# Zero matmuls beside the folding of the maxima, the row of maxima copied by bank, and TensorE's last part moved into the branch

## The chip, the cores and the metric

The kernel runs on one core of a Trainium2 chip. The core has five engines that run side by side and meet through semaphores: TensorE (matmuls, with a queue of its own for weight loads), VectorE, ScalarE, GpSimd and SyncE, which here only issues transfers. The metric is the device time of one execution in microseconds, lower is better.

## The reference

The program is one layer of a Perceiver. 128 queries of width 256 attend to a context of 12544 rows, then to themselves, and then go through a gated feed-forward part whose weights and activations are rounded to integer grids. Cut to what is computed:

```
x = x + cross_attention(layernorm(x), ctx, ctx, mask)   # 16 heads of 16, softmax over 12544 keys
x = x + self_attention(layernorm(x))                    # 16 heads of 16, causal, 128 keys
x = x + ffn(layernorm(x))                               # 256 -> 768 gate and up -> 256, quantized

# cross attention
qh, kh, vh = (q @ Wq.T + bq), (k @ Wk.T + bk), (v @ Wv.T + bv)    # each (.., 16, 16)
scores = einsum('bqhd,bkhd->bhqk', qh, kh) / 4 ; masked -> -1e7
out = einsum('bhqk,bkhd->bqhd', softmax(scores), vh)

# ffn
x = act_qdq(x);  up = act_qdq(x @ Wup.T);  gate = act_qdq(x @ Wgate.T)
gate = act_qdq(gate * round_u16(sigmoid(gate)));  o = act_qdq(gate * up);  return o @ Wdown.T
```

`act_qdq` needs the largest absolute value of its whole argument before it can round.

## The kernel before, in words

The 12544 context rows are 98 tiles of 128, in 14 blocks of 7. The order of work is written out by hand for every engine; nothing is scheduled by a planner.

**First pass** (to 244 us of the profile). For each block TensorE projects keys and values (L811, L820) and scores all queries against all keys once (L852, `score_for_max`), only to find each query's and head's largest score. VectorE takes part of these maxima straight (L626) and folds the rest, copied by ScalarE (L442), into a running array `running` of 16 heads by 448 keys (L629). Keys and values go to DRAM.

**The fold.** When the last block is scored, VectorE folds `running` by halves (L654, three steps), reduces it (L657), joins it with `row_max` (L658) and writes the negative, `neg_max` (L661). TensorE turns its 16 columns into one row of partition 96 of `ps_a`, 16 matmuls of 128 columns over four banks (L927). ScalarE copies banks 0 and 1 of that row into `q_stack` (L480), VectorE banks 2 and 3 (L665). With this row in `q_stack`, and ones in the matching row of `k_stack`, a score comes out of the matmul with the maximum already subtracted. The matmul of zeros at L934 clears `attended`, the bank in which the second pass sums.

**Second pass.** A block is 56 score matmuls in 8 units of 6 and 8 by turns (`score`, L946). Their result goes through an exponential on ScalarE (L492, four slots of probabilities) and is multiplied with the values (`add_up`, L960: 12 or 16 matmuls a unit, each of which the profile counts twice). TensorE waits for two exponentials, scores two more units, and then adds up the two. Units 14 and 15 of the last pair of blocks have nothing left to score. The loop over the pairs (L992) runs six times, and the seventh pair is written out behind it.

**The branch.** Whether any key is masked is known only at run time. TensorE loads a flag (L896) and has the two passes twice in its program, without masks and with them, each in an `If` (L996 to L998). Here nothing is masked, so the first is run. What comes behind both branches stands once: a matmul of one element (L1000) whose semaphore `sums_done` lets VectorE copy the sums (L688), four transposes of them (L1003), the normalization, the self-attention, the output projection, and the feed-forward part up to L1112.

**Zero matmuls.** `keep_clock(bank, count)` (L860 to L863) runs matmuls of zeros, 512 columns each, into a bank that nobody needs. Their counts stand in `WARM`; the first, 15, is run while VectorE normalizes the sums.

**Self-attention.** Queries and keys, then values are projected (L1020, L1028). Four groups of four heads are scored (L1036, L1038), exponentiated by ScalarE (L512, L515), turned (`turn_probs`, L1045), copied, and multiplied with the values (`attend_self`, L1053). ScalarE copies the values at L500, ahead of its first exponential.

**Feed-forward.** The peaks found by VectorE are spread over all partitions by TensorE (`spread_peaks`, L1079), and VectorE waits for them (`scales`, L743 to L749).

## Time and profile before

| | us |
|---|---|
| median of 3 timed runs | 521.67 (520.98 to 522.05) |
| the profiled execution, its own time | 524.74 |
| its span, first to last instruction | 523.0 |
| TensorE busy | 481.6 (92% of the span) |
| ScalarE busy | 375.9 (72%) |
| VectorE busy | 294.9 (56%) |
| mean granted clock of TensorE, as a share of 2.4 GHz | 0.951 |

The durations below come from the profiled execution, whose time is 3.07 us above the median of the timed runs. The times at which rows start are in us from the start of its span. A busy TensorE is not one at its peak: its matmuls are pipelined, and a row with x16 gives the time from the first start to the last end. "Idle before" in brackets names what ended the wait; "issue" means that nothing the profile shows was waited for. The granted clock of TensorE has two levels, 1.2 GHz (0.5) and 2.4 GHz (1.00); a value between them means that it changed inside the stretch. A matmul of zeros of 512 columns takes twice as long at the lower one.

### The profile page before, as it was taken

The page shows a single profiled execution, that of the slowest core. Times are in us where ns is not written, and L with a number is a line of the kernel's source. Part 1 is how long each engine was busy: PE and PEld are TensorE (multiplying, and loading weights), DVE is VectorE, ACT ScalarE, POOL GpSimd, SP SyncE. Part 2 cuts the span into 40 slices and gives each one's busy share as a digit, 9 for nine tenths or more (in the row PEclk, how much of TensorE's full clock was granted, in tenths as well). Part 3 has the DMA queues.
Part 4 walks back from the last instruction along what each step waited for, and adds up shares of the span by engine and source line. Part 5 has one row for each costly group of instructions (what it writes and reads, how often), then busy time and mean ns, then how long its engine had stood idle before and what let it go on. Part 6 is the DMA issues. An engine that isn't in the chain of part 4 may idle for free.

```text
span 523.0 us, 14251 instructions
## 1 busy us (share of the span) xinstructions
PE 481.6 (92%) x5620; PEld 381.0 (73%) x5620; DVE 294.9 (56%) x425; ACT 375.9 (72%) x410; POOL 101.2 (19%) x101
## 2 busy tenths in 40 slices
PE   6889999999999999993699999999999999959997
PEld 3867777777777776771589899898998998829443
DVE  6757999999999999999389100000000000036575
ACT  3248888888888888874489999899999999705011
POOL 5684322233332233305000000000000000000000
PEclk9879999999999999996599999999999999979699
DMA  8735676766677666958937777888777774000000
GB/s 278 248 130 205 270 303 253 266 234 230 241 291 298 237 263 233 391 233 305 410 103 275 285 269 290 303 303 301 278 267 264 262 278 170 5 3 1 0 0 10
DMA packets 34759, 117.47 MB, mean 225 GB/s; under 512 B 4400, under 2 KB 10416, under 8 KB 34736
## 3 DMA queue, kind: packets, MB, share of 16 engines
q1 hardware_dynamic: 30560, 110.58, 56.0%
q0 software_dynamic: 4032, 6.42, 4.3%
q8 instruction: 17, 0.28, 0.2%
q10 hardware_dynamic: 144, 0.13, 0.1%
q14 instruction: 6, 0.05, 0.0%
HBM read 74.44 MB, written 39.47 MB: 218 GB/s over the span
## 4 chain that ended last, share of the span: by engine, by line
PE 54%; DVE 30%; issue 10%; ACT 4%; DMA 1%; DVEq 1%; SPq 0%; ACTq 0%
PE ps_a L946 20%; PE ps_k L960 17%; DVE block_max L626 14%; DVE early L629 7%; PE ps_k L811 4%; PE ps_a L820 2%; PE ps_a L863 2%; DVE k_lo L587 2%; ACT early L442 1%; PE ps_a L852 1%; DMA v_in<-in_wv 1%; PE ps_a L1053 1%; DVE early L654 1%; PE ps_a L889 1%; PE ps_a L1091 1%
## 5 line engine op out<-in xcount | busy, mean ns | idle before, releaser
L626 DVE TENSOR_REDUCE block_max<-ps_a 128x2 f32<-128x896 f32 x112 | 121.1, 1083 | 1.8 <-PE ps_a L852 1.7
L946 PE MATMUL ps_a<-q_stack,k_stack 128*128 128x256 f32 x784 | 112.0, 295 | 1.3 <-DVE q_stack L665 0.8
L946 PEld LDWEIGHTS ps_a<-q_stack,k_stack 128*128 128x128 f32 x784 | 100.2, 192 | 13.7 <-issue 11.4
L442 ACT CAST early<-ps_a 128x896 bf16<-128x896 f32 x104 | 93.9, 903 | 8.0 <-PE ps_a L852 8.0
L492 ACT ACTIVATE middle<-ps_a 128x1536 f32<-128x1536 f32 (+1 forms) x56 | 90.3, 1663 | 13.1 <-PE ps_a L946 13.1
L688 DVE COPY early<-ps_k 128x512 f32<-128x512 f32 x1 | 0.7, 692 | 171.6 <-PE ps_a L1000 171.6
L492 ACT ACTIVATE early<-ps_a 128x1536 f32<-128x1536 f32 (+1 forms) x56 | 90.2, 1662 | 7.8 <-PE ps_a L946 7.8
L348 POOL TENSOR_TENSOR k_stack<-early,k_stack 128x448 fp32r<-128x448 f32 x52 | 59.2, 1143 | 122.6 <-DVE early L629 113.6
L820 PE MATMUL ps_a<-w_hi,k_stack 128*128 128x256 f32 x392 | 69.8, 302 | 0.0
L629 DVE TENSOR_TENSOR early<-early 128x896 bf16<-128x896 bf16 x104 | 68.0, 654 | 0.0
L811 PE MATMUL ps_k<-k_stack,w_hi 128*128 128x448 f32 x224 | 61.8, 398 | 6.2 <-DVE v_in L619 3.9
L820 PEld LDWEIGHTS ps_a<-w_hi,k_stack 128*128 128x128 f32 x392 | 54.6, 194 | 11.9 <-issue 11.7
L852 PE MATMUL ps_a<-k_hi,q_pad 32*128 32x448 f32 x448 | 54.5, 476 | 8.5 <-ACT early L442 7.7
L426 ACT ACTIVATE k_hi<-ps_k,bk 128x448 fp32r<-128x448 f32 x56 | 35.5, 634 | 32.0 <-PE ps_k L811 32.0
L811 PEld LDWEIGHTS ps_k<-k_stack,w_hi 128*128 128x128 f32 x224 | 38.7, 193 | 21.0 <-DVE k_lo L587 11.4
L960 PE MATMUL ps_k<-early,v_in 128*17 128x128 f32 x1568 | 48.2, 273 | 0.7 <-ACT early L492 0.7
L960 PE MATMUL ps_k<-middle,v_in 128*17 128x128 f32 x1568 | 48.3, 273 | 0.0
L852 PEld LDWEIGHTS ps_a<-k_hi,q_pad 32*128 32x128 f32 x448 | 22.1, 186 | 34.8 <-issue 23.4
L587 DVE SCALAR_TENSOR_TENSOR k_lo<-ps_k,bk,k_hi 128x448 fp32r<-128x448 f32 x56 | 38.1, 680 | 13.3 <-ACT k_hi L426 10.8
L960 PEld LDWEIGHTS ps_k<-early,v_in 128*17 128x17 f32 x1568 | 40.4, 97 | 4.6 <-ACT early L492 1.0
L960 PEld LDWEIGHTS ps_k<-middle,v_in 128*17 128x17 f32 x1568 | 40.4, 97 | 3.8
L432 ACT COPY early<-ps_a 128x512 f32<-128x512 f32 (+1 forms) x56 | 30.1, 537 | 15.6 <-PE ps_a L820 12.9
(172 smaller groups left out, 428.9 us busy)
## 6 DMA issues: line engine op xcount, KB each, us to landing
k_stack<-k_hi_scratch SPq DMA_DIRECT2D x56, 448.0 KB, 6.1
v_scratch<-early SPq DMA_DIRECT2D x14, 952.0 KB, 6.1
v_in<-v_scratch SPq DMA_DIRECT2D x14, 952.0 KB, 8.0
early<-in_ctx SPq DMA_DIRECT2D x14, 896.0 KB, 5.6
k_hi_scratch<-k_hi SPq DMA_DIRECT2D x28, 448.0 KB, 3.7
k_lo_scratch<-k_lo SPq DMA_DIRECT2D x28, 448.0 KB, 3.8
k_stack<-k_lo_scratch SPq DMA_DIRECT2D x28, 448.0 KB, 6.4
mask_b<-in_maskn POOLq DMA_DIRECT2D x14, 224.0 KB, 5.6
```

Source lines behind the costliest of these rows:

```text
L348: nc.gpsimd.tensor_tensor(ctx_lo[:, par, c, half], ctx_t[:, c * BK:(c + 1) * BK][:, half], ctx_hi[:, par, c, half].bitcast(f32), ALU.subtr ...
L426: nc.scalar.activation(k_hi[:, par, m, n * HK:(n + 1) * HK], ps_k[:, 0:HK], ACT.Identity, bias=bk[:, m:m + 1]).then_inc(hi_ready, 1)
L442: nc.scalar.copy(staged[:, u % 2], pair_scores(u, 0)).then_inc(max_copied, 1)
L492: nc.scalar.activation(probs[u % SLOTS_P][:, 0:width], ps_a[:, UNIT_BANK[u % 2]:UNIT_BANK[u % 2] + UP[u % 2] // 2, :].rearrange("p a n -> ...
L587: nc.vector.scalar_tensor_tensor(k_lo[:, m, half], ps_k[:, 0:HK], bk[:, m:m + 1], k_hi[:, par, m, half].bitcast(f32), ALU.add, ALU.subtrac ...
L626: nc.vector.tensor_reduce(block_max[:, par, 2 * u:2 * u + 2], pair_scores(u, 1), AX.X, ALU.max).then_inc(max_taken, 1)
L629: nc.vector.tensor_tensor(copied_rows(u), copied_rows(u), staged[:, u % 2], ALU.max).then_inc(run_taken, 1)
L811: last = nc.tensor.matmul(ps_k[:, 0:HK], w[:, 0, c, m * P:(m + 1) * P], part[:, par, c, n * HK:(n + 1) * HK], start=(k == 0), stop=(k == l ...
L820: last = nc.tensor.matmul(ps_v[:, n * D:(n + 1) * D], part[:, par, c, t * P:(t + 1) * P], w[:, 1, c, :], start=(j == 0), stop=(j == len(te ...
L852: last = nc.tensor.matmul(outs[-1], q_pad[rows, head, :], k_hi[rows, par, m, keys], start=True, stop=not masked, skip_group_check=True)
L946: last = nc.tensor.matmul(ps_a[:, bank, (k % 2) * 2 * Q:(k % 2 + 1) * 2 * Q], k_stack[:, b_par, a, t * P:(t + 1) * P], q_stack[:, a, :, :] ...
L960: last = nc.tensor.matmul(attended[32 * j:32 * j + VW, c * Q:(c + 1) * Q], v_ring[:, b_par, t, h, :], probs[slot][:, k * Q:(k + 1) * Q], s ...
```

## The change

- **The fold.** Behind the last `score_for_max` TensorE runs 24 matmuls of zeros into `attended` (`WARM_FOLD`), and then waits for `neg_max`.
- **The row of maxima.** The 16 matmuls signal after each four (one bank) and not after each eight. VectorE copies banks 0 and 2, ScalarE banks 1 and 3, 512 elements each and not 1024. The first scores wait, pair of heads by pair of heads, for the bank that holds their part of the row (`wait_max_row`), and not for the whole row.
- **The last two units.** In the last pair of blocks TensorE waits for the exponential of unit 14 before it adds up unit 14, and for that of unit 15 before it adds up unit 15, and not for both at first.
- **The end of the branch.** Everything TensorE does behind the branches stands in a function `finish()` that is called at the end of either branch. The matmul of one element is gone: VectorE waits for the last `add_up` itself (`prob_slots_free`).
- **The sums** are copied in two halves, and a half's transposes wait for that half alone.
- **The values of the self-attention** are projected behind the turning of groups 0 and 1, into bank 1 of `ps_a`, and no longer ahead of the scores. ScalarE copies them behind its third group. The values' first product now stands behind the turning of group 2, the other three behind the turning of group 3; before, two stood on either side.
- **VectorE's `scales(3, 2, 12)`** stands behind the first step on the sigmoid, and not ahead of the wait for it.

```diff
+WARM_FOLD = 24
@@ ScalarE
-            act.wait_ge(max_rows_ready, 1)
             act.wait_ge(q_spread, 8)
-            nc.scalar.mul(q_stack[SR:SR + 1, 0:PR // 2, :, :].rearrange("p a b q -> p (a b q)"),
-                          ps_a[SR:SR + 1, 0:2, :].rearrange("p a q -> p (a q)"), 1.0).then_inc(max_rows_set, 1)
+            for n in (1, 3):
+                act.wait_ge(max_rows_ready, n + 1)
+                nc.scalar.mul(q_stack[SR:SR + 1, 2 * n:2 * n + 2, :, :].rearrange("p a b q -> p (a b q)"),
+                              ps_a[SR:SR + 1, n, :], 1.0).then_inc(odd_rows_set, 1)
...
-            act.wait_ge(v2_projected, 1)
-            nc.scalar.copy(v2_sb[:, :, 0:HD], ps_k[:, D:2 * D].rearrange("p (h d) -> p h d", h=H)).then_inc(v2_copied, 1)
...
                 if g == 2:
                     copy_odd(1)
+                    act.wait_ge(v2_projected, 1)
+                    nc.scalar.copy(v2_sb[:, :, 0:HD], ps_a[:, 1, 0:D].rearrange("p (h d) -> p h d", h=H)).then_inc(v2_copied, 1)
@@ VectorE
-            dve.wait_ge(max_rows_ready, 2)
             dve.wait_ge(q_spread, 8)
-            nc.vector.tensor_scalar(q_stack[SR:SR + 1, PR // 2:PR, :, :].rearrange("p a b q -> p (a b q)"),
-                                    ps_a[SR:SR + 1, 2:4, :].rearrange("p a q -> p (a q)"), 1.0, None,
-                                    ALU.mult).then_inc(max_rows_set, 1)
+            for n in (0, 2):
+                dve.wait_ge(max_rows_ready, n + 1)
+                nc.vector.tensor_scalar(q_stack[SR:SR + 1, 2 * n:2 * n + 2, :, :].rearrange("p a b q -> p (a b q)"),
+                                        ps_a[SR:SR + 1, n, :], 1.0, None, ALU.mult).then_inc(even_rows_set, 1)
...
-            dve.wait_ge(sums_done, 1)
-            nc.vector.tensor_copy(sums_sb, attended).then_inc(sums_copied, 1)
+            dve.wait_ge(prob_slots_free, NB * UNITS + SLOTS_P)
+            for half in range(2):
+                nc.vector.tensor_copy(sums_sb[:, half * D:(half + 1) * D], attended[:, half * D:(half + 1) * D]
+                                      ).then_inc(sums_copied, 1)
...
-            scales(3, 2, 12).then_inc(up_scale_ready, 1)
             dve.wait_ge(sig_ready, 1)
             link(nc.vector.tensor_scalar(sig, sig, 65536.0, MAGIC, ALU.mult, ALU.add))
+            scales(3, 2, 12).then_inc(up_scale_ready, 1)
@@ TensorE
                 for u in range(LAG, NG):
                     score_for_max(NB - 1, 1, u, masked)
+                pe.wait_ge(lo_ready, NB * DC * 2)
+                keep_clock(attended, WARM_FOLD)
 
                 pe.wait_ge(row_max_ready, NB + 1)
...
-                    if h % HT == HT - 1:
+                    if h % 4 == 3:
                         last.then_inc(max_rows_ready, 1)
-                pe.wait_ge(lo_ready, NB * DC * 2)
                 nc.tensor.matmul(attended, zeros_b[:, 0:P], zeros_b[:], start=True, stop=True,
                                  skip_group_check=True).then_inc(prob_slots_free, SLOTS_P)
-                pe.wait_ge(max_rows_set, 2)
...
+                def wait_max_row(a):
+                    pe.wait_ge(odd_rows_set if a // 2 % 2 else even_rows_set, a // 4 + 1)
...
+                        if opening and t == 0 and a % 2 == 0:
+                            wait_max_row(a)
...
                     for u in range(0, 2 * UNITS, 2):
+                        ending = final and u == 2 * UNITS - 2
                         for w in (u, u + 1):
-                            pe.wait_ge(exp_done, i * (2 * UNITS) + w + 1)
-                            if not (final and u == 2 * UNITS - 2):
+                            if not ending:
+                                pe.wait_ge(exp_done, i * (2 * UNITS) + w + 1)
...
                         for w in (u, u + 1):
+                            if ending:
+                                pe.wait_ge(exp_done, i * (2 * UNITS) + w + 1)
                             add_up(w // UNITS, w % UNITS, w % SLOTS_P)
...
+            def finish():
+                for c in range(4):
+                    pe.wait_ge(sums_copied, c // 2 + 1)
+                    last = nc.tensor.transpose(ps_x[:, c * P:(c + 1) * P], sums_sb[:, c * P:(c + 1) * P], eye[:])
+                last.then_inc(sums_turned, 1)
...
+                turn_probs(0)
+                turn_probs(1)
+                for c in range(DC):
+                    last = nc.tensor.matmul(ps_a[:, 1, 0:D], xt[:, c, :], wqvk[:, c, D:2 * D], start=(c == 0), stop=(c == DC - 1))
+                last.then_inc(v2_projected, 1)
+                turn_probs(2)
+                pe.wait_ge(v2_copied, 1)
+                attend_self(0)
+                turn_probs(3)
+                attend_self(1)
+                attend_self(2)
+                attend_self(3).then_inc(self_attended, 1)
...
             for masked in (False, True):
                 with pe.If(masked_flag == int(masked)):
                     attend(masked)
-
-            nc.tensor.matmul(ps_v[0:1, 0:1], zeros_b[:, 0:1], zeros_b[:, 0:1], start=True, stop=True).then_inc(sums_done, 1)
-            pe.wait_ge(sums_copied, 1)
...
+                    finish()
```

What the order of the instructions shows follows for three places, all on TensorE. Lines of the changed program are a few higher: its L856 is L852 before, L867 is L863, L932 is L927, L937 is L934, L953 is L946, L967 is L960, L1009 is L1003, L1015 is L1009, L1026 is L1020, L1046 is L1045, L1054 is L1053 and L1061 is L1028.

TensorE before, between the last scoring of the first pass (L852) and the first scores of the second:

```order
L852 MATMUL ps_a<-k_hi,q_pad 128x448 x3
L927 MATMUL ps_a<-eye_b,neg_max 1x128 [waits row_max_ready]
L927 MATMUL ps_a<-eye_b,neg_max 1x128 x15
L934 MATMUL ps_k<-zeros_b 128x512 [waits lo_ready]
L946 MATMUL ps_a<-q_stack,k_stack 128x256 [waits consts_set,q_spread,stack_in0,v_evacuated,max_rows_set]
L946 MATMUL ps_a<-q_stack,k_stack 128x256 x13
```

The same place in the changed program:

```order
L856 MATMUL ps_a<-k_hi,q_pad 128x448 x3
L867 MATMUL ps_k<-zeros_b 128x512 [waits lo_ready]
L867 MATMUL ps_k<-zeros_b 128x512 x23
L932 MATMUL ps_a<-eye_b,neg_max 1x128 [waits row_max_ready]
L932 MATMUL ps_a<-eye_b,neg_max 1x128 x15
L937 MATMUL ps_k<-zeros_b 128x512
L953 MATMUL ps_a<-q_stack,k_stack 128x256 [waits stack_in0,consts_set,even_rows_set,q_spread,v_evacuated]
L953 MATMUL ps_a<-q_stack,k_stack 128x256
L953 MATMUL ps_a<-q_stack,k_stack 128x256 [waits odd_rows_set]
L953 MATMUL ps_a<-q_stack,k_stack 128x256
L953 MATMUL ps_a<-q_stack,k_stack 128x256 [waits even_rows_set]
L953 MATMUL ps_a<-q_stack,k_stack 128x256
```

The 24 matmuls of zeros now stand ahead of the 16 that wait for `neg_max`, and the wait for the whole row (`max_rows_set`) has become three here and a fourth at the start of the next unit, one for each bank.

TensorE before, at the end of the branch without masks, from the last `add_up` on:

```order
L960 MATMUL ps_k<-middle,v_in 17x128 x28
L960 MATMUL ps_k<-early,v_in 17x128 [waits exp_done]
L960 MATMUL ps_k<-early,v_in 17x128 x27
L997 UNCONDITIONAL_BRANCH
L997 COMPARE_AND_BRANCH
L811 MATMUL ps_k<-k_stack,w_hi 128x448 [waits lo_ready,q_copied,q_ready]
L811 MATMUL ps_k<-k_stack,w_hi 128x448 x3
```

The rows behind the comparison are the first pass of the branch with masks. What is run next stands some 550 rows further on, behind that branch:

```order
L960 MATMUL ps_k<-early,v_in 17x128 x27
L997 UNCONDITIONAL_BRANCH
L1000 MATMUL ps_a<-zeros_b 1x1
L1003 MATMUL ps_a<-eye,early 128x128 [waits sums_copied]
L1003 MATMUL ps_a<-eye,early 128x128 x3
L863 MATMUL ps_a<-zeros_b 128x512 x15
L1009 MATMUL ps_k<-eye,xn 128x128 [waits normed]
```

The changed program at the end of the branch without masks:

```order
L967 MATMUL ps_k<-middle,v_in 17x128 x28
L967 MATMUL ps_k<-early,v_in 17x128 [waits exp_done]
L967 MATMUL ps_k<-early,v_in 17x128 x11
L967 MATMUL ps_k<-early,v_in 17x128 [waits exp_done]
L967 MATMUL ps_k<-early,v_in 17x128 x15
L1009 MATMUL ps_a<-eye,early 128x128 [waits sums_copied] x4
L867 MATMUL ps_a<-zeros_b 128x512 x15
L1015 MATMUL ps_k<-eye,xn 128x128 [waits normed]
L1015 MATMUL ps_k<-eye,xn 128x128
```

The wait for the last exponential now divides the last `add_up`, and the transposes of the sums follow in the next row, with no branch between. The branch over the masked half stands behind the last matmul of the program.

TensorE before, in the self-attention, from the turning of group 1 on:

```order
L1045 MATMUL ps_a<-eye,middle 128x128 [waits self_exp]
L1045 MATMUL ps_a<-eye,middle 128x128 x3
L1045 MATMUL ps_k<-eye,middle 128x128 [waits self_exp]
L1045 MATMUL ps_k<-eye,middle 128x128 x3
L1053 MATMUL ps_a<-early,middle 128x17 [waits even_copied]
L1053 MATMUL ps_a<-early,middle 128x17 x3
L1053 MATMUL ps_a<-early,middle 128x17 [waits odd_copied]
L1053 MATMUL ps_a<-early,middle 128x17 x3
L1045 MATMUL ps_a<-eye,middle 128x128 [waits self_exp]
L1045 MATMUL ps_a<-eye,middle 128x128 x3
L1053 MATMUL ps_a<-early,middle 128x17 [waits even_copied]
L1053 MATMUL ps_a<-early,middle 128x17 x3
```

The changed program from the same place on:

```order
L1046 MATMUL ps_a<-eye,middle 128x128 [waits self_exp]
L1046 MATMUL ps_a<-eye,middle 128x128 x3
L1061 MATMUL ps_a<-wqvk,xt 128x256 x2
L1046 MATMUL ps_k<-eye,middle 128x128 [waits self_exp]
L1046 MATMUL ps_k<-eye,middle 128x128 x3
L1054 MATMUL ps_a<-early,middle 128x17 [waits even_copied,v2_copied]
L1054 MATMUL ps_a<-early,middle 128x17 x3
L1046 MATMUL ps_a<-eye,middle 128x128 [waits self_exp]
L1046 MATMUL ps_a<-eye,middle 128x128 x3
L1054 MATMUL ps_a<-early,middle 128x17 [waits odd_copied]
L1054 MATMUL ps_a<-early,middle 128x17 x3
L1054 MATMUL ps_a<-early,middle 128x17 [waits even_copied]
```

The projection of the values stands between the turnings of groups 1 and 2, and only one product of four heads stands ahead of the turning of group 3.

## Rows read from the trace of the kernel before

**Rows 1.** The chain of waits (start us, us, engine, tile, line).

```profile
251.94 1.88 PE ps_a L927 x16
253.84 1.24 DVE q_stack L665
255.12 3.37 PE ps_a L946 x14
258.52 1.89 ACT middle L492
260.46 1.21 PE ps_a L946 x8
...
457.18 4.18 issue
462.37 1.12 PE ps_a L1003 x4
464.45 5.12 PE ps_a L863 x15
```

**Rows 2.** The table of stretches; the column after POOL is the granted clock.

```profile
258.00:260.00 2.00, 1.92 (x9) 1.54 (x7) 0.00 (x0) 1.74 (x2) 0.00 (x0) 0.56 1.01 424
461.00:463.00 2.00, 0.79 (x4) 0.71 (x5) 0.69 (x1) 0.00 (x0) 0.00 (x0) 0.53 0.04 8
482.00:486.00 4.00, 4.00 (x18) 3.14 (x18) 0.68 (x2) 1.88 (x3) 0.00 (x0) 0.50 0.01 4
```

**Rows 3.** The timeline at the fold (start us, us, engine, line, operation).

```profile
243.40 0.75 PE L852 MATMUL ps_a<-k_hi,q_pad 32*128 32x448 f32 x4 [1.01 <-ACT early L442]
...
251.71 0.17 DVE L661 TENSOR_SCALAR neg_max<-row_max 128x16 bf16<-128x16 f32 x1
```

**Rows 4.** The timeline at the start of the program, TensorE's first zero matmuls.

```profile
1.44 6.00 PE L863 MATMUL ps_a<-zeros_b 128*128 128x512 bf16 x14 [1.44 <-POOL zeros_b L338]
```

**Rows 5.** The timeline from the last blocks to the second turning of rows.

```profile
452.09 3.22 ACT L492 ACTIVATE early<-ps_a 128x1536 f32<-128x1536 f32 x2 [0.29 <-PE ps_a L946]
...
453.01 1.72 PE L960 MATMUL ps_k<-middle,v_in 128*17 128x128 f32 x56
...
455.45 1.72 PE L960 MATMUL ps_k<-early,v_in 128*17 128x128 f32 x56 [0.72 <-ACT early L492]
...
461.36 0.17 PE L1000 MATMUL ps_a<-zeros_b 128*1 128x1 bf16 x1 [4.18 <-issue]
461.63 0.69 DVE L688 COPY early<-ps_k 128x512 f32<-128x512 f32 x1 [171.59 <-PE ps_a L1000]
...
469.83 0.42 DVE L565 COPY xt<-ps_k 128x256 f32<-128x256 f32 x1 [1.89 <-PE ps_k L1009]
```

**Rows 6.** The timeline of the self-attention.

```profile
471.06 2.56 DVE L702 TENSOR_TENSOR early<-ps_a,head_mask 128x1024 f32<-128x1024 f32 x2 [0.77 <-PE ps_a L1020]
...
472.20 1.03 PE L1028 MATMUL ps_k<-wqvk,xt 128*128 128x256 f32 x4
...
480.18 0.63 ACT L515 ACTIVATE middle<-middle 128x512 f32<-128x512 f32 x1 [0.83 <-DVE middle L722]
...
481.59 3.41 PE L1053 MATMUL ps_a<-early,middle 128*128 128x17 f32 x16
```

**Rows 7.** The timeline of the feed-forward part.

```profile
495.78 0.48 DVE L761 TENSOR_SCALAR xt<-ps_k,small 128x256 f32<-128x256 f32 x1 [0.55 <-PE ps_k L1009]
...
503.90 0.84 ACT L524 ACTIVATE early<-early 128x768 f32<-128x768 f32 x1 [19.99 <-DVE early L773]
...
505.60 0.42 DVE L746 TENSOR_REDUCE small<-ps_a 128x1 f32<-128x256 f32 x1 [0.80 <-PE ps_a L1079]
...
506.33 0.54 DVE L778 TENSOR_SCALAR early<-early 128x768 f32<-128x768 f32 x1
...
517.44 2.86 PE L1112 MATMUL ps_k<-down_w,middle 128*128 128x256 f32 x12
```

**Rows 8.** The groups of instructions by line, TensorE's scores in the second pass.

```profile
L946 PE MATMUL ps_a<-q_stack,k_stack 128*128 128x256 f32 x784 | 112.0, 295 | 1.3 <-DVE q_stack L665 0.8 <-ACT middle L492 0.5
```

196 lines of the change are left out of this document (91 added, 105 removed).

## The prediction

> **What bounds the kernel now.** I read the chain of waits first, in order of time. Up to the fold it alternates between VectorE and TensorE, and the change leaves that part alone. From 260.46 us to 457.17 us it is TensorE without a gap, and the group of scores shows only 1.3 us of idle time over all 784 of them [rows 1, 8]: the second pass runs at TensorE's pace, so what is gained at its start moves its end. Around it the chain shows the pieces that this change touches: the row of maxima and its copy, the first scores at 255.12, an exponential that holds TensorE until 260.46, and at the end "issue" for 4.18 us, the largest step of the tail [rows 1]. Then I read the granted clock by stretches. It is low (0.56) just before 260, low again (0.53) when work resumes behind the gap, and low from 482 to 486 [rows 2]. Last come the timelines, for what each step waits for.
>
> **The copy of the row and the first scores.** Before, `neg_max` is written at 251.88, the 16 matmuls take 1.88 us at the low clock, VectorE's copy 1.24 us from 253.84, and the scores start at 255.12 [rows 1, 3]. At the full clock I halve the 16 matmuls to 0.9 us, so the first bank of four is there at about 252.4. A copy of 512 elements by VectorE takes 0.69 us where 1024 took 1.24 [rows 1, 5], so bank 0 is copied at 253.1. VectorE has bank 2 to copy behind it, which makes 253.8. ScalarE's two are done by then too, if it is no slower. Scores 0 and 1 start at 253.15, unit 0 is complete at 254.3, and its exponential takes some 1.45 us: a pair takes 3.22 us [rows 5], the larger of it 1.88 [rows 1], and they overlap a little. The exponential of unit 1, the larger, follows at 255.8 and ends at 257.7, where it ended at 260.4 [rows 1]. That is 2.7 us earlier, and TensorE goes on at once.
>
> This needs the clock. If it stays low, the 14 scores take their 3.37 us [rows 1], the matmul of zeros behind the row takes 0.43 us in front of them, and the chain becomes 254.2 plus 3.4 plus 1.9: 259.5, a gain of 0.9 us. So the zero matmuls are worth 1.8 us and the banks 0.9 us.
>
> Do they end in time? A matmul of zeros takes 0.43 us at the low clock (6.00 us for 14, [rows 4]), and half of that, 0.22 us, at the full one. They start at 244.15, behind the last scoring [rows 3]. The 15 of the tail took 5.12 us [rows 1], which is 8 at 0.43 and 7 at 0.22, so the clock rose after about 3.4 us; at the start of the program 14 in a row all ran low, 6.0 us [rows 4]. With the first, 24 of them take 3.4 + 16 x 0.22 = 6.9 us and end at 251.1, ahead of `neg_max`. With the second they take 6.0 + 10 x 0.22 = 8.2 us and end at 252.35, 0.4 us behind it. I charge 0.2 us. First term: **-2.5 us**, bounds -0.9 and -2.9.
>
> **The last two units.** TensorE ends units 12 and 13 at 454.73 and then idles 0.72 us for the last exponential, while that of unit 14, the first of the two that start at 452.09, ended at 453.54 [rows 5]. Unit 14's 24 of the 56 matmuls (0.7 us) fit into that wait. Second term: **-0.7 us**, bounds 0 and -0.75.
>
> **The gap.** Between the last `add_up` at 457.17 and the matmul of one element at 461.36 nothing is waited for [rows 5]. By the order of the instructions TensorE jumps there over the whole masked branch, and it is the only long jump in the program. After the change the next row of the same stretch of code are the transposes, and VectorE starts its copy on the last `add_up`, some 0.1 us behind it, instead of at 461.63 [rows 5]. Third term: 461.63 - 457.27 = **-4.4 us**, bounds 0 (a stall of the same size at another place) and -4.4.
>
> The Trainium skill ("Runtime: NRT & Kernel Launch", Instruction fetch mechanics) says that instructions are prefetched in sequence only, and that a taken branch to a block that isn't loaded waits for its fetch. This row agrees, with 4.18 us. By the same rule the jump is not saved but moved: it now stands behind the last matmul, which is the third rival below.
>
> **The copy in halves.** Before, copy and transposes take from 461.63 to 463.49, 1.86 us, with the transposes at 1.12 us on the low clock [rows 1, 5]. Now a half takes 0.42 us (the copy at 469.83 has its size [rows 5]), the second half is there at 0.87 us, and its two transposes add about 0.4 us at the full clock. Fourth term: **-0.55 us**, bounds 0 and -0.7.
>
> **The zero matmuls of the tail.** The normalized rows are ready at 467.94 (469.83 less an idle 1.89), yet VectorE waits those 1.89 us for their transposes, because TensorE works at its 15 zero matmuls until 469.57 [rows 1, 5]. The same turning waits only 0.55 us in the feed-forward part, at the full clock [rows 7]. Without the gap the clock should never fall here, the 15 take 3.3 us against 4.45 us of VectorE work, and the wait becomes 0.55. Fifth term: **-1.3 us**, bounds 0 (if the clock falls all the same) and -1.3.
>
> **The self-attention.** The values' projection, 1.03 us, leaves its place ahead of the scores [rows 6]. These then wait for the first half of the padded queries (471.06 + 1.28 = 472.34), so they start only some 0.5 us earlier, and so does ScalarE's last exponential, which ended at 480.81 [rows 6]. But the projection now stands ahead of the turning of group 2, and behind the turning of group 3 stand three products instead of two. Two take 3.41 us at the low clock [rows 6], so about 1.7 at the full one: the third costs 0.9 us at the full clock, 1.7 us at the low. Sixth term: -0.5 + 0.9 = **+0.4 us**. Bounds: +1.2 with all three at the low clock, and -1.1 if the clock, which before was low for the two, stays high for the three.
>
> **The scale in the feed-forward part.** VectorE idles 0.80 us for TensorE ahead of 505.60, while the sigmoid was ready at 504.74 [rows 7]. The step of 0.54 us on it, which stood behind the scale at 506.33, now fits into that wait. Seventh term: **-0.5 us**, bounds 0 and -0.55.
>
> **The sum.** -2.5 - 0.7 - 4.4 - 0.55 - 1.3 + 0.4 - 0.5 = -9.55 us. For the profiled execution that makes 524.74 - 9.55 = 515.2 us. The timed runs lie 3.07 us below it; as the terms are waits and not shares, I take the same difference from their median: 521.67 - 9.55 = 512.1 us.
>
> **The rivals.**
>
> *The clock does not follow.* The zero matmuls don't raise it in time, or it falls again while TensorE waits for the copies. For: between 252 and 260 TensorE was busy most of the time, and the clock still rose only shortly before 260 [rows 2]. Against: the zero matmuls are denser than that. The first term shrinks to 0.9 or less: 512.1 + 1.7 = 513.8 us. If the tail stays low too, the fifth term goes and the fourth shrinks: 515.3 us.
>
> *The stall stays, in front of new code.* If TensorE has to wait for instructions behind the last `add_up` in any case, the third term goes, and the clock falls in the wait, so the fifth goes with it: 512.1 + 4.2 + 1.3 = 517.6 us. Against: code was run in sequence from 428 us on, in the last pair of blocks, with no such gap in the chain [rows 1].
>
> *The jump moves to the end.* TensorE's last matmul ended at 517.44 + 2.86 = 520.30 [rows 7], and the span at 523.0. If TensorE jumps only then, it is done 4.2 us later, at 524.5, 1.5 us behind the output: 513.6 us. Against: TensorE's instructions are issued ahead of its matmuls, and 12 of 0.24 us give a lead of more than 1.5 us, in which case it costs nothing. The rule of the skill cited above, by which that branch has to fetch, would give this result.
>
> *Slower than before.* The body of the loop over the pairs of blocks (L992) now stands 48 instructions further on (24 matmuls, each with its weight load). If the body, now cut differently by the blocks in which instructions are held, is no longer held as a whole, each of its five jumps back pays the price of the long jump, 4.2 us: 21 us, and 512.1 + 21 = 533 us. It decides from the first jump back that has to wait; three of the five would be enough to be slower. Against: before, the group of scores has no idle "issue" at all [rows 8], and the body itself is as long as before.
>
> The skill's page gives TensorE room for 2048 instructions; the body has some 1140 by the order, so by it the loop would fit wherever it stands.
>
> **How the numbers follow.** Forecast as above 0.60; clock 0.15; jump at the end 0.14; stall stays 0.07; slower 0.02; something not seen, without gain, 0.02. The likeliest is 512.1 us. Its own terms spread by about 1.5 us to either side: the bounds of the self-attention reach 1.5 us below, and those of the fold and the fifth term above. To reach the clock's and the end's cases the range goes up to 515.3; below, to 510.0. It leaves out the stalled and the slower case. A measurement of this kernel can tell a change of about 0.2%, 1 us. Faster by more than that holds in all cases but two, which with a margin makes 0.95; within it 0.02; slower 0.03.
>
> **What would show it.** In the changed profile: the granted clock at 1.00 by 252 us; two copies of 512 elements on VectorE and two on ScalarE; the second exponential of the pass ending near 257.7; the last `add_up` split in 24 and 32 with no wait over 0.1 us between units 13 and 14; VectorE's first half copy within 0.2 us of the last `add_up`; the 15 zero matmuls in 3.3 us; a wait of 0.55 us for the second turning; a span of about 513.4 us with the profiled execution's own time 1.7 us above it. If that difference is 3 us, the jump has moved to the end. The forecast is wrong if the chain shows "issue" of over 1 us behind the last `add_up`, or the clock at 0.5 in the first scores.

## The result and the profile after

| | before | after |
|---|---|---|
| median of the first comparison, 4 runs each | 521.86 us (520.98 to 522.22) | 513.82 us (513.47 to 514.36) |
| ratio, 95% interval | | 0.983 (0.9809 to 0.985) |
| second comparison, 11 and 5 runs | 522.76 us (521.27 to 525.20) | 513.86 us (511.88 to 514.25) |
| ratio, 95% interval | | 0.9807 (0.9778 to 0.9837) |
| span of the profiled execution | 523.0 us | 512.2 us |
| its own time | 524.74 us | 513.95 us |

The change makes the kernel faster, by 8.0 us in the first comparison and 8.9 in the second; the forecast was 512.1 us, a gain of 9.55. For the profiled execution it was 515.2 us, with a span of about 513.4; measured were 513.95 and 512.2. In the profiled executions the span shrank by 10.8 us. The difference between these figures is the first question that the experiments take up. The median by itself tells little of the mechanism: 513.8 us was also the time of the rival in which the clock does not follow at the fold, and 513.6 that of the jump moved to the end. What sets them apart is in the rows.

The place of the fold and the first scores, in the timeline of the changed kernel (start us, us, engine, line, operation, what ended the idle time before):

```profile
243.56 7.99 PE L867 MATMUL ps_k<-zeros_b 128*128 128x512 bf16 x24
...
251.18 0.17 DVE L663 TENSOR_SCALAR neg_max<-row_max 128x16 bf16<-128x16 f32 x1
...
251.47 1.05 PE L932 MATMUL ps_a<-eye_b,neg_max 128*1 128x128 bf16 x16
...
251.97 1.31 DVE L668 TENSOR_SCALAR q_stack<-ps_a 1x512 fp32r<-1x512 f32 x2 [0.61 <-PE ps_a L932]
...
252.81 1.97 PE L953 MATMUL ps_a<-q_stack,k_stack 128*128 128x256 f32 x14
253.87 3.22 ACT L494 ACTIVATE middle<-ps_a 128x1536 f32<-128x1536 f32 x2 [0.62 <-PE ps_a L953]
```

By the profile the 24 zero matmuls end at 251.55, 0.2 us behind `neg_max` (251.35); the 16 matmuls of the row start at 251.47, 0.12 us behind it, where it was 0.06 before. The 16 matmuls of the row now take 1.05 us, where they took 1.88 [rows 1]. VectorE's copies start four matmuls into the row, the scores start at 252.81, 1.46 us behind `neg_max` where it was 3.24 [rows 1, 3], and the second exponential ends at 257.09.

The tail, from the last exponentials to the feed-forward part, in the same view:

```profile
448.78 3.22 ACT L494 ACTIVATE early<-ps_a 128x1536 f32<-128x1536 f32 x2 [0.29 <-PE ps_a L953]
...
449.69 1.72 PE L967 MATMUL ps_k<-middle,v_in 128*17 128x128 f32 x56
...
451.23 1.88 PE L967 MATMUL ps_k<-early,v_in 128*17 128x128 f32 x56
...
453.25 0.76 DVE L691 COPY early<-ps_k 128x256 f32<-128x256 f32 x2 [163.70 <-PE ps_k L967]
...
453.73 0.77 PE L1009 MATMUL ps_a<-eye,early 128*128 128x128 f32 x4 [0.62 <-DVE early L691]
...
454.34 3.40 PE L867 MATMUL ps_a<-zeros_b 128*128 128x512 bf16 x15
...
459.01 0.44 PE L1015 MATMUL ps_k<-eye,xn 128*128 128x128 f32 x2 [1.27 <-DVE xn L563]
...
459.49 0.42 DVE L567 COPY xt<-ps_k 128x256 f32<-128x256 f32 x1 [0.53 <-PE ps_k L1015]
...
459.97 3.27 PE L1026 MATMUL ps_a<-xt,wqvk 128*128 128x128 f32 x16 [0.52 <-DVE xt L567]
...
474.74 0.26 DVE L732 RECIPROCAL stats<-ps_a 128x16 f32<-128x16 f32 x1 [3.58 <-PE ps_a L1054]
...
485.48 0.48 DVE L765 TENSOR_SCALAR xt<-ps_k,small 128x256 f32<-128x256 f32 x1 [0.55 <-PE ps_k L1015]
...
495.38 0.42 DVE L750 TENSOR_REDUCE small<-ps_a 128x1 f32<-128x256 f32 x1 [0.34 <-PE ps_a L1085]
```

The rows to set beside those of before [rows 5 to 7]: the last `add_up` starts as the one before it ends, with no idle time; VectorE copies 0.14 us behind its end (453.11) and not 4.46 us behind; the zero matmuls take 3.40 us and not 5.12; VectorE waits 0.53 us for the second turned rows and not 1.89. One row is worse: the 16 projections at 459.97 take 3.27 us, where they took 2.05 before. The granted clock, the column behind POOL in the table of stretches, says why:

```profile
252.00:254.00 2.00, 2.00 (x20) 1.64 (x18) 1.28 (x2) 1.20 (x3) 0.00 (x0) 1.00 1.07 442
457.00:463.00 6.00, 4.21 (x22) 3.36 (x21) 3.42 (x10) 0.37 (x1) 0.00 (x0) 0.80 0.00 0
```

It is at 1.00 in the first scores, as wanted, and was low until almost 260 before [rows 2]. But between 457 and 463 it is 0.80: it fell in the projections, after TensorE had idled 1.27 us between the end of the zero matmuls (457.74) and the turning (459.01).

VectorE's last row of the timeline:

```profile
509.51 0.48 DVE L802 SCALAR_TENSOR_TENSOR x<-ps_k,small,x 128x256 f32<-128x256 f32 x1 [2.25 <-PE ps_k L1118]
```

From the end of that row (509.99) to the end of the span (512.2) it is 2.2 us, as before.

### The profile page after: what moved, and what is told of

It is laid out like the page before. It is cut to its first block, busy times and chain, and to the rows that moved or that the text cites. A ratio compares the mean times of both kernels' runs of the same rounds, so it can differ in the third digit from the quotient of the medians.

```text
span 512.2 us, 14299 instructions
## 1 busy us (share of the span) xinstructions
PE 484.1 (95%) x5643; PEld 380.3 (74%) x5643; DVE 294.8 (58%) x427; ACT 375.8 (73%) x411; POOL 101.1 (20%) x101
## 4 chain that ended last, share of the span: by engine, by line
PE 61%; DVE 22%; issue 8%; ACT 5%; DMA 2%; POOL 1%; DVEq 0%; SPq 0%; ACTq 0%; POOLq 0%
PE ps_a L953 20%; PE ps_k L967 18%; DVE block_max L628 10%; PE ps_k L815 6%; DVE early L631 5%; PE ps_a L824 4%; PE ps_a L856 3%; ACT early L443 3%; PE ps_k L867 2%; DMA early<-in_ctx 1%; DMA v_in<-in_wv 1%; DVE k_lo L589 1%; PE ps_a L1039 1%; PE ps_a L1054 1%; PE ps_a L893 1%
## 5 line engine op out<-in xcount | busy, mean ns | idle before, releaser
L953 PE MATMUL ps_a<-q_stack,k_stack 128*128 128x256 f32 x784 | 110.1, 291 | 1.4 <-ACT middle L494 1.4
L953 PEld LDWEIGHTS ps_a<-q_stack,k_stack 128*128 128x128 f32 x784 | 98.3, 188 | 13.5 <-issue 11.6
L856 PE MATMUL ps_a<-k_hi,q_pad 32*128 32x448 f32 x448 | 54.5, 475 | 8.6 <-ACT early L443 7.7
L967 PE MATMUL ps_k<-early,v_in 128*17 128x128 f32 x1568 | 48.4, 273 | 0.0
L967 PE MATMUL ps_k<-middle,v_in 128*17 128x128 f32 x1568 | 48.2, 273 | 0.0
L856 PEld LDWEIGHTS ps_a<-k_hi,q_pad 32*128 32x128 f32 x448 | 22.0, 186 | 35.0 <-issue 23.6
L589 DVE SCALAR_TENSOR_TENSOR k_lo<-ps_k,bk,k_hi 128x448 fp32r<-128x448 f32 x56 | 38.0, 678 | 13.3 <-ACT k_hi L427 10.8
L967 PEld LDWEIGHTS ps_k<-early,v_in 128*17 128x17 f32 x1568 | 40.4, 97 | 3.9 <-ACT early L494 0.3
L967 PEld LDWEIGHTS ps_k<-middle,v_in 128*17 128x17 f32 x1568 | 40.4, 97 | 3.8
```

The costliest lines, as they stand in the source:

```text
L589: nc.vector.scalar_tensor_tensor(k_lo[:, m, half], ps_k[:, 0:HK], bk[:, m:m + 1], k_hi[:, par, m, half].bitcast(f32), ALU.add, ALU.subtrac ...
L856: last = nc.tensor.matmul(outs[-1], q_pad[rows, head, :], k_hi[rows, par, m, keys], start=True, stop=not masked, skip_group_check=True)
L953: last = nc.tensor.matmul(ps_a[:, bank, (k % 2) * 2 * Q:(k % 2 + 1) * 2 * Q], k_stack[:, b_par, a, t * P:(t + 1) * P], q_stack[:, a, :, :] ...
L967: last = nc.tensor.matmul(attended[32 * j:32 * j + VW, c * Q:(c + 1) * Q], v_ring[:, b_par, t, h, :], probs[slot][:, k * Q:(k + 1) * Q], s ...
```

## The experiments

All are changes of one of the two kernels, timed beside the kernel before, in three groups whose medians of the kernel before are 523.40, 522.76 and 523.15 us. Medians of different groups are therefore compared only roughly. Since the first 250 us turned out to vary, the profiles are compared by stretches, with `neg_max` as the start of the first; each stretch is seen in one profile.

### The kernel before, once more

No edit.

> The kernel before, unchanged, in a new profiled execution. The spans fell by 10.8 us (523.0 to 512.2), the medians by 8.0 (521.86 to 513.82). Theory A: the first profiled execution of before was itself some 3 us slower than its timed runs, somewhere outside the places that the change touches; then this one has a span near 520.1 us (the median less 1.74), the long jump again at 4.2 us, the scores again 3.2 us behind neg_max, and the 3 us are missing between other rows. Theory B: the waits that the change removes are shorter in most executions (the jump nearer 2 us, or the tail at the full clock), so the change gains less there than in the first profile; then the jump or the tail is shorter here by 2 to 3 us. Time of the kernel: 521.9 either way.

Measured: 523.45 us (521.84 to 525.03, 12 runs), and 523.40 (521.18 to 524.86) in the 17 runs beside it. The profiled execution has a span of 520.2 us. The stretches of the first 40 us, first profile of before, then the new one:

```profile
0.00:20.00 20.00, 15.53 (x58) 10.66 (x59) 11.75 (x23) 7.26 (x10) 11.00 (x14) 0.83 0.78 252
20.00:40.00 20.00, 15.87 (x96) 12.55 (x94) 12.90 (x18) 7.80 (x11) 15.78 (x12) 0.83 0.56 194
```

```profile
0.00:20.00 20.00, 15.58 (x70) 10.63 (x71) 12.90 (x25) 8.64 (x11) 11.02 (x14) 0.91 0.80 259
20.00:40.00 20.00, 15.87 (x103) 12.33 (x102) 13.80 (x19) 8.42 (x13) 15.81 (x12) 0.91 0.66 236
```

And `neg_max` in the new one:

```profile
249.03 0.17 DVE L661 TENSOR_SCALAR neg_max<-row_max 128x16 bf16<-128x16 f32 x1
```

It is written at 249.20 instead of 251.88 [rows 3], 2.7 us earlier, and the spans differ by 2.8; from `neg_max` on the two take 271.0 and 271.1 us. Theory A holds as to the place: the difference lies in the first pass, with the clock high for more of the first 40 us (0.91 against 0.83). All twelve profiles of this case go the same way, and none of the edits touches the first pass. With a mean clock of 0.83 in the first 40 us `neg_max` is written between 250.95 and 251.97 (seven profiles), with 0.87 at 250.47 and 250.72, with 0.91 at 249.20, 249.75 and 249.77. From `neg_max` on, the waits that the change removes differ little between the two profiles: the gap to VectorE's copy is 4.20 us and not 4.46, the wait for the second turned rows 1.58 and not 1.89, and the self-attention takes 0.31 us longer. What theory A had not said is that neither execution is unusual. Over 53 runs the kernel before goes from 520.93 to 525.20, with a median of 523.15. The first comparison had four of them, from the lower half.

### The changed kernel, once more

No edit.

> The changed kernel, unchanged, timed beside the kernel before once more. 17 more runs of the kernel before went from 521.2 to 524.9, with a median of 523.4, and in its second profile neg_max was written 2.7 us earlier than in the first, with the clock high for more of the first 40 us (0.91 against 0.83) and every later stretch of the same length. Theory A (the 8.0 us of the first comparison are too few, since its four runs of before were of the quick sort): 513.5 to 514.5 beside a before of 523.4, ratio 0.981 to 0.982, a gain of 9.5 us. Theory B (the change gains less in most executions than in the profiled ones): ratio 0.984 or more.

Measured: 513.86 us (511.88 to 514.25), ratio 0.9807 (0.9778 to 0.9837). Theory A's ratio (0.981 to 0.982) is as good as met; theory B's 0.984 lies just outside this interval, though inside that of the first comparison. Against all 53 runs of before the nine runs of the changed kernel (median 513.86) are 9.3 us faster. From `neg_max` on, its new profile takes 261.0 us, the first 260.85, and the kernel before 271.1 and 271.0: a gain of 10.2 us there. The other 0.9 us, between this and the 9.3 of the medians, would have to lie ahead of `neg_max`, in the part that varies; no run separates it.

### The jump kept

```diff
             for masked in (False, True):
                 with pe.If(masked_flag == int(masked)):
                     attend(masked)
-                    finish()
+            finish()
```

> The changed kernel with finish() called once behind both branches, so that TensorE jumps over the masked half again; VectorE still copies the sums on the last add_up. Theory (the jump is the largest term): the transposes start 4.2 us behind the last add_up plus a bit, where they start 0.6 us behind it; 3.7 us. The clock falls in that wait, so the transposes take 1.1 instead of 0.8 us and the 15 zero matmuls hold TensorE until 1.3 us behind the normalized rows: 5.2 us in all, 519.0. The projections behind it run at the full clock again, which gives back up to 1.2 us: 517.8. Rival (the stall has only moved to the end of the program, where its price is paid in part): 2 to 3 us slower only, 516.

Measured: 515.58 us (514.97 to 516.32), span 514.0. The timeline behind the last `add_up`:

```profile
453.92 0.76 DVE L691 COPY early<-ps_k 128x256 f32<-128x256 f32 x2 [164.18 <-PE ps_k L967]
...
457.21 0.66 PE L1009 MATMUL ps_a<-eye,early 128*128 128x128 f32 x4 [3.43 <-issue]
...
457.70 5.09 PE L867 MATMUL ps_a<-zeros_b 128*128 128x512 bf16 x15
```

The jump costs 3.43 us of idle time here, and VectorE copies the sums within it. The sums are turned 3.99 us behind the start of the copy and not 1.29: 2.7 us later, and not 3.7. The zero matmuls take 5.09 us, as in the kernel before, and the second turned rows are copied 0.2 us later by that (a wait of 0.72 us and not 0.53). But then the projections run at the full clock, and from there to the reciprocal of the self-attention it is 13.75 us and not 15.25. The sum is +2.7 + 0.2 - 1.5 = +1.4 us; the output projection behind it takes 0.26 us less, and from `neg_max` to the end of the span it is 262.0 us, +1.2. The medians differ by 1.7. Both predictions of the expectation were too high; its rival was nearer, though not for its reason: nothing was paid at the end of the program.

This run also says why the zero matmuls cost so much in the kernel before. There they start late, behind a second idle time in which nothing is waited for:

```profile
464.45 5.12 PE L863 MATMUL ps_a<-zeros_b 128*128 128x512 bf16 x15 [0.96 <-issue]
```

That is 0.92 us behind the start of the reciprocal of the turned sums (463.53), and the second profile of the kernel before shows the same 0.96 and 0.93 us. Here they start 0.21 us ahead of that reciprocal. They last as long (5.09 us), yet the wait for the turned rows is 0.72 us and not 1.89. So the low clock alone costs 0.2 us of the 1.35; the rest needs the late start as well. By estimate the late start alone would have cost nothing: 464.45 and 3.40 us make 467.85, ahead of the normalized rows at 467.94. What TensorE waits for in those 0.96 us no run says; they are gone in every kernel changed here.

### Only the branch

The kernel before, with its last part (the matmul of one element included) called inside either branch.

```diff
+            def finish():
+                nc.tensor.matmul(ps_v[0:1, 0:1], zeros_b[:, 0:1], zeros_b[:, 0:1], start=True, stop=True).then_inc(sums_done, 1)
+                ...
             for masked in (False, True):
                 with pe.If(masked_flag == int(masked)):
                     attend(masked)
-            nc.tensor.matmul(ps_v[0:1, 0:1], ...
+                    finish()
```

> The kernel before with one edit: all that stood behind the branches is called at the end of either branch (the matmul of one element too). Theory from the terms of the forecast: the gap of 4.18 us goes (4.2), and as the clock doesn't fall in it, the transposes lose 0.35 us and the wait of 1.9 us behind the zero matmuls becomes 0.55 (1.3): 5.8 us below the kernel before. But the 15 zero matmuls then end 1.2 us ahead of the normalized rows, the clock falls in the projections as in the changed kernel, and that takes 1.2 us back: 4.6 us below. Rival, from the run with the jump kept, which was only 1.7 us slower than the changed kernel: 2 to 3 us below.

Measured: 516.74 us (516.00 to 516.98), 6.0 us below the 522.76 beside it, ratio 0.9875 (0.9851 to 0.99). The timeline:

```profile
453.92 1.72 PE L960 MATMUL ps_k<-early,v_in 128*17 128x128 f32 x56 [0.74 <-ACT early L492]
...
455.44 0.17 PE L997 MATMUL ps_a<-zeros_b 128*1 128x1 bf16 x1
455.80 0.69 DVE L688 COPY early<-ps_k 128x512 f32<-128x512 f32 x1 [167.50 <-PE ps_a L997]
...
457.04 3.40 PE L863 MATMUL ps_a<-zeros_b 128*128 128x512 bf16 x15
...
461.71 0.44 PE L1006 MATMUL ps_k<-eye,xn 128*128 128x128 f32 x2 [1.27 <-DVE xn L561]
...
462.19 0.42 DVE L565 COPY xt<-ps_k 128x256 f32<-128x256 f32 x1 [0.53 <-PE ps_k L1006]
...
462.67 2.05 PE L1017 MATMUL ps_a<-xt,wqvk 128*128 128x128 f32 x16 [0.52 <-DVE xt L565]
```

The gap is gone: the matmul of one element is issued while the last `add_up` still drains, and VectorE starts 0.16 us behind its end. The zero matmuls run at the full clock, and the wait for the turned rows is 0.53 us. From the last `add_up` to the second turned rows this is 6.55 us, against 12.66 before [rows 1, 5]: 6.1 us, of which 4.3 are the gap, 0.46 the copy and transposes and 1.35 the wait behind the zero matmuls. TensorE idles the same 1.27 us as in the changed kernel, but the clock did not fall in the projections (2.05 us), so the part that the expectation took back stayed. It fell in the last products (0.77 from 474 to 476), and the stretch to the reciprocal of the self-attention takes 14.30 us, 0.9 less than before. From `neg_max` to the end the profile gains 7.1 us, the medians 6.0.

### No zero matmuls beside the fold

```diff
-WARM_FOLD = 24
+WARM_FOLD = 0
```

> The changed kernel without the 24 zero matmuls beside the fold. Theory: the clock stays low until the second pass has run for some us, the 16 matmuls take 1.9 instead of 1.05 us and the first 14 scores 3.4 instead of 2.0 us, so the second exponential ends 1.8 us later: 515.6. Rival 1: the clock is worth nothing there, since the first scores wait for the copies in any case and the exponentials have the same length: 513.8 to 514.2. Rival 2: the zero matmuls end behind neg_max in most executions (0.1 us in the profile) and cost what they give: 513.8 or less.

Measured: 514.15 us (513.90 to 515.08), against 513.8 for the changed kernel.

```profile
250.78 0.17 DVE L663 TENSOR_SCALAR neg_max<-row_max 128x16 bf16<-128x16 f32 x1
...
251.11 1.87 PE L932 MATMUL ps_a<-eye_b,neg_max 128*1 128x128 bf16 x16 [7.88 <-DVE neg_max L663]
...
254.83 3.22 ACT L494 ACTIVATE middle<-ps_a 128x1536 f32<-128x1536 f32 x2 [1.23 <-PE ps_a L953]
...
460.00 0.44 PE L1015 MATMUL ps_k<-eye,xn 128*128 128x128 f32 x2 [1.27 <-DVE xn L563]
...
460.95 2.05 PE L1026 MATMUL ps_a<-xt,wqvk 128*128 128x128 f32 x16 [0.52 <-DVE xt L567]
```

From `neg_max` (250.95) to the end of the second exponential (258.05) it is 7.10 us instead of 5.74: 1.36 us, not the 1.8 of the theory. The pair of exponentials starts at 254.83 and takes 3.22 us, as with the clock high. In the self-attention 0.96 us came back (14.29 us and not 15.25): behind the same idle 1.27 us the clock did not fall in the projections this time, but in the last products (0.87 from 472 to 474). So the median looked like rival 1, and the profile showed most of the theory's loss, offset by a gain 200 us later. No row ties that gain to the missing zero matmuls.

### 20 zero matmuls in the tail

```diff
-WARM = (15, 13, 8, 10, 14, 18, 6, 2)
+WARM = (20, 13, 8, 10, 14, 18, 6, 2)
```

> The changed kernel with 20 zero matmuls in place of 15 beside the normalization of the sums. In the changed profile the 15 end at 457.74, TensorE idles 1.27 us, and the clock falls at 460.56, in the projections, which take 3.27 instead of 2.05 us. Theory: 20 of them end at 458.8, ahead of the normalized rows (458.95), the clock doesn't fall there, and 1 to 1.2 us are won: 512.7. Rival: the clock falls later instead, in the first scores or products of the self-attention, and nothing is won: 513.8. Where the clock doesn't rise in time they hold TensorE beyond the normalized rows and cost up to 1 us: 514.8.

Measured: 512.01 us (511.52 to 512.29), ratio to before 0.9784 (0.9768 to 0.9799), 1.8 us below the changed kernel, more than the theory gave (512.7). From `neg_max` to the end of the span it is 259.4 us and not 260.85, 1.4 us less.

```profile
454.05 4.48 PE L867 MATMUL ps_a<-zeros_b 128*128 128x512 bf16 x20
...
459.20 0.42 DVE L567 COPY xt<-ps_k 128x256 f32<-128x256 f32 x1 [0.53 <-PE ps_k L1015]
...
459.68 2.05 PE L1026 MATMUL ps_a<-xt,wqvk 128*128 128x128 f32 x16 [0.52 <-DVE xt L567]
...
472.95 0.26 DVE L732 RECIPROCAL stats<-ps_a 128x16 f32<-128x16 f32 x1 [3.40 <-PE ps_a L1054]
```

They end at 458.53, ahead of the turning, which waits for VectorE as it should; the projections take 2.05 us and not 3.27, and from the second turned rows to the reciprocal it is 13.75 us and not 15.25.

### 26 zero matmuls in the tail

```diff
+WARM = (26, 13, 8, 10, 14, 18, 6, 2)
```

> The changed kernel with 26 zero matmuls beside the normalization. At the full clock they take 5.6 us and end 1.1 us behind the normalized rows (4.6 us after the turned sums), so VectorE waits some 1.7 instead of 0.53 us for the second turned rows. Theory: the clock stays high, and the kernel takes 512.0 + 1.1 = 513.1 us; that is also why the 15 of the kernel before, at the low clock, cost 1.35 us. Rival: TensorE's idle time, not the order, decides; the wait stays at 0.5 us and the time at 512.0.

Measured: 513.05 us (512.53 to 513.86).

```profile
460.24 0.42 DVE L567 COPY xt<-ps_k 128x256 f32<-128x256 f32 x1 [1.42 <-PE ps_k L1015]
```

The wait for the turned rows is 1.42 us where it was 0.53, and what follows is 13.76 us, with the clock high. The theory's time is met (its wait of 1.7 us was a little too long), and its rival is out. 20 zero matmuls end 4.28 us behind the start of the reciprocal of the turned sums and leave the wait at 0.53 us; 26 end 5.58 us behind it, later than VectorE's normalized rows (4.41 us behind it), and hold them up.

### No zero matmuls at the fold, 20 in the tail

Both edits above.

> The changed kernel with 20 zero matmuls beside the normalization and none beside the fold, to be compared with the one that has both (512.0 us). Without the fold's alone the kernel took 514.15 where the changed one took 513.8: 0.3 us, though its profile lost 1.36 us between neg_max and the end of the second exponential; it won 0.96 us back in the self-attention, where the clock did not fall ahead of the projections. Theory: that gift was the tail's, which 20 zero matmuls give to both kernels; now the full 1.4 us show: 513.4, and from neg_max to the end of the span 260.8 us against 259.4. Rival: the fold's zero matmuls are worth no more than 0.3 us in the median of executions: 512.3.

Measured: 514.22 us (512.90 to 514.87), 2.2 us above the kernel that has both sets, which was timed in another group. From `neg_max` to the end of the second exponential it is 6.79 us (5.68 with both), and from there on 1.1 us more is lost in the self-attention, 14.89 us against 13.75; from `neg_max` to the end of the span it is 261.7 us against 259.4. One stretch of this profile:

```profile
470.00:474.00 4.00, 4.00 (x30) 3.96 (x29) 0.23 (x1) 2.37 (x4) 0.00 (x0) 0.78 0.02 4
```

The clock fell at the last products, 0.78 over this stretch and 0.97 with both sets; the last 24 products take 3.89 us, with both sets 2.75. TensorE had idled only 0.19 us ahead of the turning here, so 20 zero matmuls do not secure the clock up to the last products. The fold's zero matmuls are worth 1.1 to 1.4 us at their place. Of the 1.1 us behind, the runs don't say whether they belong to them or to where the clock happened to turn.

### The row copied whole

The signals behind eight matmuls, 1024 elements for each engine, one wait for both copies.

```diff
-            for n in (0, 2):
-                dve.wait_ge(max_rows_ready, n + 1)
+            dve.wait_ge(max_rows_ready, 2)
...
-                        if opening and t == 0 and a % 2 == 0:
-                            wait_max_row(a)
```

> The changed kernel with the row of maxima copied as before: signals after eight matmuls, 1024 elements by each engine, and the scores wait for both copies. Theory: with the clock high the row is complete 1.05 us after its start, VectorE's copy of 1.23 us begins there and not after four matmuls, the scores start at 253.9 instead of 252.8 and nothing of the row is late behind them; the first exponential starts 0.85 us later and everything with it: 514.7 if the kernel is at 513.8. Rival: the first exponential started at 253.87 in the changed kernel only because bank 2 was copied last, so that copying the banks whole delays it by less than 0.5 us: 514.2.

Measured: 513.79 us (513.51 to 515.31), where the changed kernel beside it took 513.86. The profile:

```profile
249.60 0.17 DVE L662 TENSOR_SCALAR neg_max<-row_max 128x16 bf16<-128x16 f32 x1
...
250.99 1.23 DVE L666 TENSOR_SCALAR q_stack<-ps_a 1x1024 fp32r<-1x1024 f32 x1 [1.22 <-PE ps_a L930]
...
252.47 4.24 PE L949 MATMUL ps_a<-q_stack,k_stack 128*128 128x256 f32 x20 [1.27 <-DVE q_stack L666]
...
255.76 1.88 ACT L493 ACTIVATE middle<-ps_a 128x2048 f32<-128x2048 f32 x1 [0.26 <-PE ps_a L949]
```

```profile
248.00:252.00 4.00, 2.42 (x22) 1.26 (x20) 2.68 (x5) 1.02 (x1) 0.00 (x0) 1.00 1.07 421
252.00:256.00 4.00, 3.53 (x16) 3.43 (x17) 0.22 (x1) 1.69 (x2) 0.00 (x0) 0.57 1.01 424
```

Here the scores start 2.70 us behind `neg_max`, not 1.46, and the clock fell behind TensorE's wait of 1.27 us for the copies: 0.57 from 252 to 256. The second exponential ends 7.87 us behind `neg_max` and not 5.74. From `neg_max` to the end of the span it is 263.3 us, 2.5 more than in the changed kernel. But this execution's `neg_max` came 1.6 us early, and the medians are equal. With a spread of 1.8 to 2.4 us in either set of five runs, the medians neither confirm nor exclude the 0.9 us that the expectation gave to the banks at the full clock (514.7 against 513.8).

### The old order of the self-attention

The changed kernel with 20 zero matmuls in the tail; values projected ahead of the scores and copied first, two products ahead of the turning of group 3 and two behind it.

```diff
+                for c in range(DC):
+                    last = nc.tensor.matmul(ps_k[:, D:2 * D], xt[:, c, :], wqvk[:, c, D:2 * D], ...)
...
-                attend_self(0)
-                turn_probs(3)
-                attend_self(1)
+                for g in range(3):
+                    turn_probs(g)
+                attend_self(0)
+                attend_self(1)
+                turn_probs(3)
```

> The changed kernel with 20 zero matmuls beside the normalization (512.0 us) and the order of the self-attention as before: values projected ahead of the scores, two products on either side of the turning of group 3. From the copy of the second turned rows to the reciprocal of the self-attention it was 15.2 us in the kernel before, 15.25 in the changed one, and 13.75 where the clock stayed high (with 20 zero matmuls, and with the jump kept). Theory: the order by itself is worth little, and the 1.5 us are the clock; with the old order and the clock high it is 13.5 to 14.0 us, and the kernel stays at 511.8 to 512.2. Rival: the new order starts the scores 0.6 us earlier and that is what is gained: 14.4 us here, 512.6. If the clock falls ahead of the last products, they take 3.4 instead of 1.9 us: 513.5.

Measured: 511.74 us (510.95 to 512.45), against 512.01 with the new order.

```profile
457.91 0.42 DVE L567 COPY xt<-ps_k 128x256 f32<-128x256 f32 x1 [0.53 <-PE ps_k L1015]
...
471.75 0.26 DVE L732 RECIPROCAL stats<-ps_a 128x16 f32<-128x16 f32 x1 [2.94 <-PE ps_a L1057]
```

13.84 us with the old order and the clock high, 13.75 with the new one. The order is worth nothing that can be measured; where the clock stayed high until near the end of the stretch it takes 1.4 to 1.5 us less than in the changed kernel.

## Why the forecast was right

The stretches of the first two profiles, from rows of the chain and the timelines, with the term of the forecast beside each:

| stretch | before | after | difference | forecast |
|---|---|---|---|---|
| `neg_max` to the end of the second exponential | 8.52 | 5.74 | -2.78 | -2.5 |
| to the end of the last `add_up` | 196.77 | 196.02 | -0.75 | -0.7 |
| to the start of VectorE's copy of the sums | 4.46 | 0.14 | -4.32 | -4.4 |
| to the reciprocal of the turned sums | 1.90 | 1.29 | -0.61 | -0.55 |
| to the copy of the second turned rows | 6.30 | 4.95 | -1.35 | -1.3 |
| to the reciprocal of the self-attention | 15.21 | 15.25 | +0.04 | +0.4 |
| to the feed-forward part's turned rows | 10.74 | 10.74 | 0 | 0 |
| to VectorE's last instruction | 24.56 | 24.03 | -0.53 | -0.5 |
| to the end of the span | 2.66 | 2.69 | +0.03 | 0 |
| sum | 271.1 | 260.85 | -10.3 | -9.55 |

- **The copy of the row and the first scores.** The size of the whole holds, and so does the mechanism; the division between its two parts was off. The zero matmuls delayed the row by 0.06 us, less than the 0.2 that was charged. (The forecast's count of 8 slow and 7 fast ones in the tail gives 5.0 us and not 5.12; nearly 9 were slow.) Of the 2.8 us, taking the zero matmuls away costs 1.1 to 1.4; the forecast had given them 1.8. What is left without them is 8.52 less 7.10 or 6.79, 1.4 to 1.7 us, where I had worked out 0.9 for the banks: I had the clock low through all 14 first scores (3.37 us), and in these two profiles it rose within them (0.75 and 1.00 from 254 to 256, where it was 0.50 before), and they took 2.94 and 2.48 us. The banks' part at the full clock stays open.
- **The last two units** came out as worked out. So did the size of **the copy in halves**, but most of it is the clock: with the sums copied whole and the transposes at the full clock this stretch takes 1.44 us, 0.46 less than before, and the halves add 0.15.
- **The gap** and **the zero matmuls of the tail.** Shown by the kernel before with this edit alone: 5.65 us in the two stretches (4.3 and 1.35), for the 5.7 of the two terms; with what came along in the transposes and the self-attention the profile gains 7.1 us and the medians 6.0. The gap's term holds. The wait's 1.35 us has the right size, but the forecast put it down to the low clock alone, as did the expectation of the run with 26. The jump kept shows that 5.09 us of zero matmuls cost only 0.2 us where they start in time; before, they also started 0.96 us late, which the forecast left out. The same run showed that the gap is not a fixed price added to all else: as soon as VectorE may copy meanwhile, the jump costs 2.7 us of the path.
- **The self-attention.** Here the step failed, though for the changed kernel its bounds held. I weighed an order of instructions (+0.9 for a third product behind the turning, -0.5 for earlier scores), and the measured worth of the order is about 0.1 us. What decided was the clock, which I had reckoned with only for the last products. In the changed kernel these do run at the full clock (24 in 2.9 us), but it fell ahead of them, in the projections. The 15 zero matmuls now last 3.40 us and leave TensorE idle for 1.27 us, a hole that the fifth term's numbers (3.3 us against 4.45) contained and that I did not follow up. I had written that the clock should never fall here. The two errors cancelled, and that the term came out near its size is luck.
- **The hole as a cause.** It is not the whole cause. In all five profiles that have it (the changed kernel twice, the row copied whole, no zero matmuls at the fold, only the branch) the clock fell before the reciprocal, but at two places: in the projections in the first three (3.27 to 3.62 us for them, 15.25 to 15.60 for the stretch), in the last products in the other two (14.29 and 14.30). Of the five without it, four take 13.75 to 13.84 us, and one, without the fold's zero matmuls, 14.89. What decides the place the runs don't show. With the clock high the stretch of the self-attention shrinks by 1.46 us, more than the lower bound of -1.1. That bound was itself added up wrong: three products at the full clock are 2.55 us, 0.85 below the 3.41 of before, which with -0.5 makes -1.35.
- **The scale** gave its 0.5 us: the wait of 0.80 us [rows 7] is 0.34 now.
- **The jump at the end.** The rival is out. The profiled executions' own times lie 1.74 us above the span before and 1.75 us after. If TensorE, now with a long jump behind its last matmul, had been late at the end, that difference would have grown. The Trainium skill's rule ("Runtime: NRT & Kernel Launch", Instruction fetch mechanics) that a taken branch to code not loaded waits for a fetch agrees with the idle times where the jump stands on the path: 4.18 and 3.93 us in the two profiles of before, 3.43 with the jump kept. That a fetch fills them no row shows, and whether TensorE waits at all behind its last matmul none shows either; if it does, it costs no time.
- **Slower than before** is out as well: the second pass takes 196.0 us from the second exponential on, as before less the last unit, so the jumps back of its loop cost nothing.
- **The time.** Where the measured gain fell short of the sum in the first comparison, 8.0 against 9.55 us, most of it lies with the four runs of before, whose median is 1.3 us under that of all 53 (a spread of 4.3 us). The chosen difference of 3.07 us between the profiled execution and the median was itself a reading of three quick runs. Against the 53 runs the gain is 9.3 us. That it lies so near 9.55 is partly luck: from `neg_max` on the profiles gain 10.2 us.

## What to carry to other kernels

Zero matmuls that keep the clock have to be counted for the clock at which they will run: when an edit in front of them kept the clock high, the same 15 lasted 3.40 us instead of 5.12, and the hole behind them gave back part of the gain (going from 15 to 20 won 1.4 us by the profile, 1.8 by the medians; 26 lost 1.0 again). Code behind an `If` that is run once is worth copying into the branch when a long jump stands on the path, and an engine that waits only for the result should wait for the result itself, not for an instruction behind the jump. Before a gain is judged by a median, look at how far the unchanged part of the kernel moves between executions, and compare stretches that start behind it.
